# Twelve products that nothing reads are dropped around the attention's lead, and the loads of one head move from the setup into the attention

## The reference

```python
mod = jax.nn.silu(c) @ w_adaln + b_adaln
sh_msa, sc_msa, g_msa, sh_mlp, sc_mlp, g_mlp = jnp.split(mod, 6, axis=-1)
h = _modulate(_ln(x), sh_msa, sc_msa)
qkv = (h @ w_qkv + b_qkv).reshape(B, N, 3, nh, hd).transpose(2, 0, 3, 1, 4)
q, k, v = (qkv[0], qkv[1], qkv[2])
attn = jax.nn.softmax(jnp.einsum('bhqd,bhkd->bhqk', q, k) * hd ** (-0.5), axis=-1)
o = jnp.einsum('bhqk,bhkd->bhqd', attn, v).transpose(0, 2, 1, 3).reshape(B, N, C)
o = o @ w_proj + b_proj
x = x + g_msa[:, None, :] * o
...
topk_logits, topk_idx = jax.lax.top_k(gate_logits, TOP_K)
...
return x + g_mlp[:, None, :] * moe
```

## Time and profile before

| what | value |
| --- | --- |
| median of 3 runs | 882.88 us (880.33 to 883.78) |
| the profiled execution, its own time | 879.99 us |
| its span (first to last instruction) | 878.2 us |
| setup, up to the barrier | about 0 to 64.5 us |
| lead of the attention | about 64.5 to 98 us |
| steps of the attention | about 98 to 446 us |
| mixture of experts, TensorE at work | about 554 to the end |

### The profile page before, as it was taken

How to read it: one execution, slowest core, us unless ns; L and a number is a source line. 1 busy time by engine, 2 the same in 40 slices (tenths; PEclk the granted TensorE clock), 3 DMA queues, 4 the chain that set the end, 5 groups by cost and what they waited for, 6 DMA issues and landing times. The chain is left out here.

```text
span 878.2 us, 16928 instructions
## 1 busy us (share of the span) xinstructions
PE 807.6 (92%) x5995; PEld 549.8 (63%) x5995; DVE 559.7 (64%) x986; ACT 480.0 (55%) x971; POOL 307.4 (35%) x297
## 2 busy tenths in 40 slices
PE   4979999999999999999999872699999999999994
PEld 2765544434444433443435641699999999999994
DVE  5668879997677988999933868155454444444441
ACT  2541568887666877888885663344333333333331
POOL 5746200000221001003820780565554434444432
PEclk9999999999999999999999995799999999999998
DMA  9021302422030212224124951443322222221211
GB/s 262 5 57 32 75 2 59 128 59 54 8 88 23 64 41 48 57 50 122 56 68 133 282 189 56 116 121 63 79 43 39 42 39 44 37 46 35 47 26 20
DMA packets 48858, 61.93 MB, mean 71 GB/s; under 512 B 16324, under 2 KB 42802, under 8 KB 48276
## 3 DMA queue, kind: packets, MB, share of 16 engines
q1 hardware_dynamic: 39635, 47.70, 19.6%
q0 software_dynamic: 8400, 12.12, 8.4%
q10 hardware_dynamic: 745, 1.04, 0.4%
HBM read 32.73 MB, written 15.46 MB: 55 GB/s over the span
## 5 line engine op out<-in xcount | busy, mean ns | idle before, releaser
L1132 DVE TENSOR_REDUCE negmax<-m_ps 128x2 f32<-128x1024 f32 x256 | 301.4, 1220 | 48.9 <-PE m_ps L1210 47.4
L1089 ACT ACTIVATE probs<-s_ps 128x512 f32<-128x512 f32 x495 | 269.5, 605 | 49.0 <-PE o_ps L1269 37.0
L1249 PE MATMUL s_ps<-stack 56*128 56x512 f32 x495 | 167.3, 467 | 1.6 <-ACT proj_f L1081 0.6
L1269 PE MATMUL o_ps<-probs,v_aug 128*19 128x256 f32 (+1 forms) x1952 | 158.3, 396 | 2.9 <-ACT probs L1089 1.4
L1210 PE MATMUL m_ps<-stack 54*128 54x512 f32 x512 | 139.5, 446 | 0.0
L1249 PEld LDWEIGHTS s_ps<-stack 56*128 56x128 f32 x495 | 71.0, 184 | 102.5 <-ACT probs L1089 90.4
L2130 PE MATMUL gate_bank<-weights,ht_hi 128*128 x630 | 127.1, 296 | 0.4 <-DVE ht_lo L2026 0.4
L2106 PE MATMUL h_ps<-weights,xt_hi 128*128 x525 | 115.4, 351 | 4.7 <-DVE xt_hi L2019 4.7
L1852 ACT CAST ht_hi<-ht_ps 128x384 fp32r<-128x384 f32 x105 | 43.5, 488 | 117.9 <-PE ht_ps L2117 117.9
L1804 POOL DMA_INDIRECT out<-res,ido x35 | 56.9, 1627 | 138.7 <-DVE res L2048 138.4
L2130 PEld LDWEIGHTS gate_bank<-weights,ht_hi 128*128 128x128 f32 x630 | 101.4, 189 | 0.6 <-issue 0.6
(11 more groups left out here) (223 smaller groups left out, 1055.1 us busy)
## 6 DMA issues: line engine op xcount, KB each, us to landing
stack<-parts SPq DMA_DIRECT2D x81, 144.0 KB
w_raw<-in_L_cond_w SPq DMA_DIRECT2D x9, 432.0 KB, 4.0
w_raw<-in_L_cond_w SPq DMA_DIRECT2D x9, 384.0 KB, 3.3
xn_scratch<-h SPq DMA_DIRECT2D x16, 192.0 KB, 1.9
x_in<-in_x SPq DMA_DIRECT2D x4, 576.0 KB, 8.8
o_scratch<-o_norm SPq DMA_DIRECT2D x16, 144.0 KB, 2.4
o_in<-o_scratch SPq DMA_DIRECT2D x16, 144.0 KB, 3.4
xr<-in_x SPq DMA_DIRECT2D x16, 144.0 KB, 4.2
```

What stands on the lines that cost most here:

```text
L1089: nc.scalar.activation(probs[:, st % 2, h], score_bank(k), ACT.Exp, scale=SCALE)\
L1132: nc.vector.tensor_reduce(negmax[:, half, first:first + count], m_ps[n % 2][:], AX.X, ALU.max, negate=True)\
L1249: nc.tensor.matmul(score_bank(k), stack[s][r, j, 1, kt // QT, (kt % QT) * P:(kt % QT + 1) * P], stack[s][r, j, 0, half], start=True, stop= ...
L1269: mm = nc.tensor.matmul(o_ps[h * HP:h * HP + HA, cols], v_aug[:, tile, (g % NG) * GH + h], probs[:, st % 2, h, cols], start=(kt == 0 and p ...
```

## The change

The two calls of `busy` and the function are dropped. The loads of head 2 of `stack[0]` go from the end of SyncE's list in the setup to the head of its list in the attention. Nothing else changes.

```diff
@@ setup, block.sync
-            heads.load_stack(sp, 0, (0, 1, 2))
+            heads.load_stack(sp, 0, (0, 1))
@@ attention, block.sync
+            heads.load_stack(sp, 0, (2,))
             heads.load_stack(sp, 1, (0, 1))
             load_rows_of_max(sp, 0, 0, (0,))
             heads.load_stack(sp, 1, (2, 3))
@@ attention, block.tensor
-            def busy(bank, count):
-                for _ in range(count):
-                    nc.tensor.matmul(s_ps[bank][0:7 * HD], wqk[0][:, 0, 0:7 * HD], heads.x[0][:, 0, 0:HALF], start=True,
-                                     stop=True)
-
             def busy_at_end(count):
...
-            busy(0, 6)
             for i, it in enumerate(plan.lead):
                 item(*it)
...
             pe.wait_ge(slot_free, LEAD_SLOTS + 1)
-            busy(LEAD_SLOTS % S_BANKS, 6)
             score(0, 0)
```

## The result

| | median, us | executions, us |
| --- | --- | --- |
| before, timed beside the change | 883.33 | 880.33, 882.88, 883.78, 894.06 |
| with the change | 892.45 | 888.18, 892.17, 892.74, 893.57 |

The ratio is 1.0105, with an interval of 1.0054 to 1.0156: about 1% slower, where 0.5% faster had been forecast. One of the four executions of before, 894.06, is no slip. With the later runs 93 executions of that kernel were timed beside the experiments, and they fall into two groups with nothing between: 44 at 878.3 to 884.4 and 49 at 890.0 to 894.9. The change has one group: all of its 16 executions (these four and the twelve of the tenth experiment) lie at 888.2 to 893.8.

The account below looks back on a forecast made before the run. VectorE was taken to bound the lead's projections, TensorE its value blocks and the steps. The lead's start gives 3.9 - 0.5 = 3.4 us, its end 1.5, together 4.9: 878.0 us from a median of 882.88, range 873.5 to 882.0.

Parts of the forecast that it names:

- The barrier: Ahead of the lead: with six transfers in place of nine, SyncE is done 3.46 us earlier.
- A wait that comes to light: At the first maxima: TensorE waits for heads 0 and 1 until about 63.6; gain 3.9 us, bounds 3.4 and 5.7.
- TensorE's clock: Start of the lead: clock falls to half, then recovers on the lead's own products; costs 0.5 us, bounds 0 to 1.2.
- rival C: In the lead: clock stays low, rounds lose 15 us, net 10 us slower, 893; chance 0.06.
- the first block: Six unread products between barrier and first maxima: they take 2.82 us, which dropping them saves if nothing else holds the maxima.
- Cover: In the lead: waits for the first projection's weights and for head 2 stay hidden, head 2's by 2 us; cost nothing.
- The six products behind the lead: Between the lead's last maxima and `score(0, 0)`: dropping them gains 1.5 us, bounds 0.7 and 1.6.
- rival A: Both ends of the lead: covers were needed, clock back late, maxima's rows late; gain only 2.9 us, 880.0; chance 0.22.

Follow-up runs that it names:

- the tenth experiment: The change again, unaltered, against many executions of the kernel before: median 890.96 us, ratio 1.0045.
- The eleventh experiment: The change, with the loads of heads 2 and 3 held back until projection unit 4 is split: one execution, 890.4 us.
- 1: Kernel before with only head 2's loads moved behind the barrier, both unread blocks kept: median 892.2 us, ratio 1.0066.
- 8: Kernel before with head 2 moved, 15 unread products at the setup's end and 20 behind the barrier: median 879.34 us, ratio 0.9932.
- 2: Kernel before with only the six unread products ahead of the lead dropped: median 891.47 us, ratio 1.0103.
- 4: Kernel before with both unread blocks dropped, three heads still loaded in the setup: median 890.55 us, ratio 1.0029.
- 5: Kernel before with 16 unread products in place of 6 ahead of the lead: median 885.11 us, ratio 1.0007.
- 6: Kernel before with 28 unread products in place of 10 at the end of the setup: median 880.45 us, ratio 0.9929.
- 7: Kernel before with 28 unread products at the setup's end and the six behind the lead dropped: median 882.33 us, ratio 0.9958.
- the fourteenth trace: Kernel before, unchanged, traced a third time: 888.19 us.
- ninth: Kernel before with head 0 on SyncE, head 1 on ScalarE, heads 2 and 3 behind the barrier, unread products filling the wait: median 879.41 us, ratio 0.993.
- the twelfth run: Kernel before, unchanged, traced once more: 881.39 us.

## Why the prediction was wrong

**The barrier: right.** 3.3 us earlier; 3.46 was predicted.

**A wait that comes to light: the mechanism right, the size wrong.** TensorE waits for heads 0 and 1, as said, but until 12.06 us after the first transfer, not 9.5. The gain at the first maxima was 1.3 us, not 3.9, below the lower bound of 3.4. The step that failed is the reading of the earlier trace rows: that 234 packets had moved by 63.5 us was taken to mean that these were transfers 1 to 6, and landed. Nine were in the queue, and the count mixes them. In that very trace head 1's semaphore has its last event at 65.15, 11.0 us after the first transfer, so that even undisturbed the gain could not pass 2.3 us. The eleventh experiment, with six alone, has its 234th packet at 66.0 - 55.37 = at most 10.6 us, the last event at 11.1 and the first maxima at 11.25. The rest of the change's 12.06 goes with the other heads' transfers: the last event comes at 11.8 to 12.2 us in the four traces in which heads 2 and 3 are issued 7.1 to 7.3 us after the first transfer (the change, 1, 8, 10), and at 11.0 to 11.6 in the ten with three heads in the setup.

**TensorE's clock: the step that decided, and wrong by a factor of 24.** "I take 0.5", bounds 0 to 1.2; measured 12.07 us from first to last maxima. The prediction had the fall right, and what it costs a round: 1.77 us was computed, and 1.87 to 2.30 measured. It had the end of the fall wrong, since it gave the lead's own products the power that it read into the earlier trace rows, and cast out rival C with the words that at half clock TensorE "has no pauses and works as unbroken as it did from 64.67 to 69.46". Both halves of this fail. The weight loads of the rounds stand idle twice in each, which the matmul rows hide. And so they did in the trace of before, ahead of the rise at 69.46, once the six unread products were over:

```profile
67.49 0.50 PEld L1210 LDWEIGHTS m_ps<-stack 54*128 54x128 f32 x4 [0.65 <-issue]
68.64 0.50 PEld L475 LDWEIGHTS s_ps<-stretch,wqk_hi 128*126 128x126 f32 x2 [0.65 <-issue]
```

The "4.8 us of unbroken products" were 2.8 us of them and then the lead's own. What the runs showed in place of the step: without unread products right ahead of it, the lead does not bring the clock back. In every trace in which it began so at half clock, it stayed there for 28 us or more: the change, 2, 4, 10, 11. Rival C at 893 was what happened, at a chance of 0.06. Its parts were off against each other, so that its sum came close partly by luck: 15 us of loss less 4.9 of gain, measured 12.07 less 2.99.

The Trainium skill, "TensorE: Matmul & The Clock Gate", section "A second HAM failure mode: psum-queue depth-cycling", says that small idle times between groups of products can make the clock swing between its two levels. The traces here show no swinging: 0.50 in every stretch of the change from 68 to 101 us, and in the trace of before 1.00 with the same rounds from 70 to 96 us. Nor does activity of any kind release the clock at once, as the prediction had put the page's rule: in the change it came back only after 32 us of the lead's products.

**What the first block was worth.** The prediction priced it at the 2.82 us that it takes. The groups of executions show its real worth. Without it, none of 40 executions (the change, 2, 4 and 10) lies under 886.7; with it, 44 of 93 lie at 878.3 to 884.4. With 16 products, or with no idle time ahead, none of 24 lies above 887.2 (5 and 6). The block buys, about every second time, a lead at full clock, which is worth some 11 us. The profile of before and all three times shown with it were of the lower group, so a view of it could show that the clock came back, but not by how little.

**Cover: right.** No wait for the first projection's weights or for heads 2 and 3 shows in the rows of the change. The slow lead asks for them late, though; the better test is the eighth run, whose lead has the full clock and takes 28.01 us from first to last maxima, against 28.03 in the sixth without the move.

**The six products behind the lead: right in the change, not in general.** 1.68 saved against 1.5 predicted, which is luck. The reading of the earlier trace rows had the same fault as that of the earlier trace rows: the packets of the first pair had moved by 95.75, but its semaphore has its last event at 97.05, 1.2 us behind the last maxima. In the change, after a slow lead, it comes 1.2 us ahead of them (108.17 against 109.37). In kernels whose lead is at full clock the rows are as late as rival A feared (0.4 and 0.7 us saved, below the bound of 0.7 or at it), and the clock falls in the first steps, of which the prediction did not think: 1.9 us lost net (7 against 6).

**Open.** Why the lead does not bring the clock back is not shown. The pauses may be the reason, but no run took them away. Against them as the only reason: the fourteenth trace and that of before have the same pauses behind the six products, and the clock came back in one of them alone; and at full clock a round has pauses too, shorter (0.36 and 0.24 to 0.25 us ahead of the weight loads from 70 to 76 us in the trace of before), and holds its clock. The kind of products is an untested rival: those of the maxima have 54 rows, the unread ones 128. Also open: what decides in which executions of the kernel before six products suffice; why six transfers need over 10 us.

**A better version.** The eighth and ninth take 879.3 and 879.4 us, with no execution above 881.5; they keep unread work up to the first maxima or to within 0.34 us of them, and both traces show the full clock throughout the lead. That is 2 us under before's lower group (medians 881.2 to 881.8) and 13 under its upper one (892.6 to 893.4).

## What to carry to other kernels

Before an unread product is dropped, ask what state the engine is in when the real work begins, and read the rows of the weight loads too, because joined matmul rows show a broken round as busy 1.00. When a transfer has landed is told by its semaphore, or by the engine that waits for it, and not by the packets that its queue has moved: that reading was wrong twice here, by 1.65 and by 1.3 us. If the clock falls in the idle time ahead of a stage of short, waiting rounds, fill that time up to the first real product; a block with a wait of 3.30 us behind it (1) did nothing for the stage. And time more than a handful of executions when a clock is in play: three times within 3.5 us of each other hid a second group 11 us above.

## What the runs showed of the hardware

One program, with the same idle time and the same products behind it, got the full clock back after 4.8 us of products in one execution and not within 29 us in another (the earlier trace rows and the fourteenth run). Where it did come back, it took from 2.9 us after the first unread product (the twelfth run) to 5.5 (the fifth, with 16). The Trainium skill, "TensorE: Matmul & The Clock Gate", section "What's actually happening", says that the slow phase varies from run to run and that its cost is under 1% of a typical span. The first agrees; the second does not, since 11 us of 881 are over 1.2%, and they are lost in one stage.

Six transfers of 144 KB in one queue let TensorE go on only 11.25 us after the first was issued, though one of that size elsewhere in the program (`o_scratch<-o_norm`) lands in 2.4 us. The first three, head 0's, report last at 7.5 to 7.6 us in every trace with one queue, so the price is there from the start; as three and three in two queues, the second of which began 3.3 us behind the first (9), it was 10.3.
